# Cross attention: another order of its five slots

## What is computed

```python
def _L0_xattn_ref(query, key, value, Wq, bq, Wk, bk, Wv, bv, Wo, bo):
    q = (query @ Wq.T + bq).reshape(b, -1, H, HD).transpose(0, 2, 1, 3)
    k = (key @ Wk.T + bk).reshape(b, -1, H, HD).transpose(0, 2, 1, 3)
    v = (value @ Wv.T + bv).reshape(b, -1, H, HD).transpose(0, 2, 1, 3)
    scores = jnp.einsum('bhqd,bhkd->bhqk', q, k) / jnp.sqrt(jnp.float32(HD))
    attn = jax.nn.softmax(scores, axis=-1)
    out = jnp.einsum('bhqk,bhkd->bhqd', attn, v)
    out = out.transpose(0, 2, 1, 3).reshape(b, -1, D)
    return out @ Wo.T + bo
...
x = x + _L0_xattn_ref(_layernorm(x, axis=-1), ctx_1024, ctx_1024, L0_xattn_Wq, L0_xattn_bq, L0_xattn_Wk, L0_xattn_bk, L0_xattn_Wv, L0_xattn_bv, L0_xattn_Wo, L0_xattn_bo)
...
```

## Time and profile before

| | us |
|---|---|
| median of 3 runs | 3766.26 (3761.07 to 3767.85) |
| the profiled execution, own time | 3766.18 |
| its span | 3764.2 |
| the eight iterations of cross attention | about 77 to 629 of the span |
| one middle iteration | 71.69 |

### The profile page before, as it was taken

How to read it: one execution, slowest core, us unless ns; L and a number is a source line. 1 busy time by engine, 2 the same in 40 slices (tenths; PEclk the granted TensorE clock), 3 DMA queues, 4 the chain that set the end, 5 groups by cost and what they waited for, 6 DMA issues and landing times. The chain is left out here.

```text
span 3764.2 us, 57324 instructions
## 1 busy us (share of the span) xinstructions
PE 3529.5 (94%) x21008; PEld 2858.3 (76%) x21008; DVE 2305.5 (61%) x5002; ACT 1523.1 (40%) x3973; POOL 1185.7 (31%) x1044
## 2 busy tenths in 40 slices
PE   5889987899999997999999969999999699999998
PEld 4666665688888885888888858888888588888887
DVE  4776775799999994333323239999999642223231
ACT  4655663455555553211111125555555431111111
POOL 2333342455555540111111125555555111111111
PEclk8999999899999998999999989999999899999999
DMA  4111122212221114111111131222111221111111
GB/s 130 39 40 53 60 71 70 97 60 62 69 65 61 60 46 142 66 62 62 62 62 62 51 106 49 65 66 61 60 60 57 88 92 65 64 64 64 64 65 56
DMA packets 220778, 253.72 MB, mean 67 GB/s; under 512 B 33337, under 2 KB 147778, under 8 KB 220501
## 3 DMA queue, kind: packets, MB, share of 16 engines
q1 hardware_dynamic: 220501, 250.07, 20.4%
HBM read 142.62 MB, written 90.61 MB: 62 GB/s over the span
## 5 line engine op out<-in xcount | busy, mean ns | idle before, releaser
L1691 DVE SCALAR_TENSOR_TENSOR u_full<-banks,b_cols,gate 128x512 f32<-128x512 f32 (+1 forms) x176 | 132.1, 750 | 889.3 <-ACT gate L1633 792.8
L45 PE MATMUL banks<-fxT_h,w_h 128*128 128x512 f32 (+1 forms) x1408 | 558.2, 396 | 4.9 <-DVE fxT_l L1683 4.9
L47 PE MATMUL banks<-fxT_h,w_l 128*128 128x512 f32 (+1 forms) x1408 | 557.6, 396 | 0.0
L46 PE MATMUL banks<-fxT_l,w_h 128*128 128x512 f32 (+1 forms) x1408 | 556.3, 395 | 0.0
L1633 ACT ACTIVATE gate<-banks,b_cols 128x512 f32<-128x512 f32 (+1 forms) x176 | 121.2, 689 | 1028.7 <-PE banks L47 1028.7
L1021 POOL TENSOR_TENSOR rn<-ssq,neg_half 128x8 f32<-128x8 f32 x128 | 210.8, 1647 | 424.3 <-DVE ssq L1295 417.6
L45 PE MATMUL banks<-wqkv_h,hT_h 128*128 128x512 f32 x768 | 322.6, 420 | 16.4 <-DVE wqkv_l L1282 16.4
L1230 ACT ACTIVATE pT_h<-banks 128x384 fp32r<-128x384 f32 x512 | 223.8, 489 | 277.1 <-PE banks L1118 276.7
L1339 DVE TENSOR_SCALAR prob<-prob,rc 128x384 f32<-128x384 f32 x512 | 324.3, 675 | 9.1
L45 PEld LDWEIGHTS banks<-fxT_h,w_h 128*128 128x128 f32 (+1 forms) x1408 | 260.5, 185 | 75.5 <-DVE fxT_l L1683 10.9
L1223 ACT ACTIVATE prob<-neg_s,neg_m 128x384 f32<-128x384 f32 x512 | 310.9, 617 | 6.8 <-DVE neg_m L1327 6.8
(11 more groups left out here) (174 smaller groups left out, 8326.6 us busy)
## 6 DMA issues: line engine op xcount, KB each, us to landing
y_in<-y_rows SPq DMA_DIRECT2D x64, 256.0 KB, 3.0
z_rows<-y_in SPq DMA_DIRECT2D x64, 256.0 KB, 2.0
f_res<-z_rows SPq DMA_DIRECT2D x16, 1024.0 KB, 5.7
f_x<-x_rows SPq DMA_DIRECT2D x16, 1024.0 KB, 8.1
y_rows<-f_res SPq DMA_DIRECT2D x16, 1024.0 KB, 4.3
out_rows<-f_x SPq DMA_DIRECT2D x16, 1024.0 KB, 4.8
w_ffn_stage<-in_w SPq DMA_DIRECT2D x30, 512.0 KB, 4.6
x_in<-in_x SPq DMA_DIRECT2D x10, 1024.0 KB, 6.7
```

The costliest lines, as they stand in the source:

```text
L45: pe.matmul(out, a_h, b_h, start=start, stop=False)
L46: pe.matmul(out, a_h, b_l, start=False, stop=False)
L47: return pe.matmul(out, a_l, b_h, start=False, stop=stop)
L1691: e.scalar_tensor_tensor(out=u_full[r, m % 2, :], in0=ps[r, 2 * (m % 2), :], scalar=b1[r, m, 0:1], in1=gate[r, :], op0=ALU.add, op1=ALU.mu ...
```

## The change

The same instructions are issued, in another order within the slots, on four engines:

- TensorE: `queries(2)` moves from slot (0, 3) to (0, 1), and the four `project` each one slot later, to (0, 2), (0, 3), (0, 4), (1, 0) (the last stays); `queries(3)` moves from (1, 3) to (1, 1), and the next iteration's `queries(0)` and `queries(1)` from (2, 3) and (3, 3) to (2, 1) and (3, 1). The four `transpose_x` move from (1, 4), (2, 0), (2, 1), (2, 2) to (1, 2), (1, 3), (1, 4), (2, 0).
- ScalarE: `hi_p` always stands ahead of `exps` of its slot; `hi_q` moves from the end of slot 3 to the head of slot 2.
- VectorE: `lo_o` stands ahead of the maximum in slot 1 and `lo_q` ahead of that of slot 2; `moments` moves from (3, 0), (3, 2) to (3, 2), (3, 4), `normalise` from (0, 4), (1, 2) to (0, 1), (0, 2), `finish` from (1, 3), (1, 4) to (1, 4), (2, 1), `add_x1` and `moments_y` by up to a slot.
- GpSimd: `root` stands ahead of the first division of an iteration.

```diff
@@ tensor
-                            if (q, k) == (0, 1) and not g.first:
+                            if (q, k) == (0, 1):
+                                queries(2, q_out(2))
+                            elif (q, k) == (0, 2) and not g.first:
...
-                            elif (q, k) == (1, 3):
+                            elif (q, k) == (1, 1):
                                 queries(3, q_out(3) if g.first else w_out(4))
...
-                            elif (q, k) == (2, 3) and not g.last:
+                            elif (q, k) == (2, 1) and not g.last:
                                 queries(0, x_out(4))
-                            elif (q, k) == (3, 3) and not g.last:
+                            elif (q, k) == (3, 1) and not g.last:
                                 queries(1, q_out(5))
@@ scalar
-                            if k == 0 and q != 2 and more:
-                                exps(it, q + 1, k)
                             if k == 1 and not (g.first and q == 0):
                                 hi_o(it, q - 1)
+                            if k == 2 and (q < 2 or not g.last):
+                                hi_q(it, q + 2)
                             hi_p(it, QK * q + k)
...
+                            if k < GT and more:
                                 exps(it, q + 1, k)
-                            if k == 3 and (q < 2 or not g.last):
-                                hi_q(it, q + 2)
@@ vector
-                            if (q, k) in ((1, 3), (1, 4)) and old:
-                                for tt in ((0, 1) if k == 3 else (2, 3)):
+                            if (q, k) in ((1, 4), (2, 1)) and old:
+                                for tt in ((0, 1) if q == 1 else (2, 3)):
                                     finish(it - 1, g.slot(-1), tt)
-                            if q == DC - 1 and k in (0, 2) and not g.last:
-                                moments(g.slot(2), g.round(2), (0, 1) if k == 0 else (2, 3))
+                            if q == DC - 1 and k in (2, 4) and not g.last:
+                                moments(g.slot(2), g.round(2), (0, 1) if k == 2 else (2, 3))
```

More of the change, by code:

```diff
@@ L444, in body @@
                 def body(g, s):
+                    if not (g.first or g.last):
+                        root(g.it + 1)
                     for q in range(DC):
@@ L450, in body @@
                                 add_bias(g.it + 1, g.slot(1), 2 * (q - 2) + k)
-                            if q == 0 and k == 0 and not (g.first or g.last):
-                                root(g.it + 1)
                             if q == 1 and k == 1 and not g.first:
@@ L584, in body @@
                                 values(it, m - 2)
-                            if (q, k) == (1, 4) and not g.last:
-                                transpose_x(it + 1, 0, TURNS, q_out(4))
                 def nothing():
@@ L762, in body @@
                         for k in range(QK):
-                            x1_of = {(0, 2): 0, (0, 3): 1, (1, 0): 2, (1, 1): 3}.get((q, k))
+                            x1_of = {(0, 3): 0, (0, 4): 1, (1, 0): 2, (1, 1): 3}.get((q, k))
                             if x1_of is not None and old:
                                 add_x1(it - 1, g.slot(-1), x1_of, TURNS)
-                            if k == 1 and q == 0 and old:
+                            if k == 1 and (q or old):
                                 lo_o(it, q - 1)
+                            if k == 2 and (q < 2 or not g.last):
+                                lo_q(it, q + 2)
                             if k < GT and more:
                                 maxima(it, q + 1, k)
-                            if k == 1 and q:
-                                lo_o(it, q - 1)
                             if 0 < k < GT and more:
@@ L775, in body @@
                             lo_p(it, QK * q + k)
[L776 to L789, removed]
-                            if (q, k) in ((1, 3), (1, 4)) and old:
-                                for tt in ((0, 1) if k == 3 else (2, 3)):
+                            if (q, k) in ((1, 2), (1, 3), (1, 4), (2, 0)) and not g.last:
+                                lo_x(it + 1, {(1, 2): 0, (1, 3): 1, (1, 4): 2, (2, 0): 3}[q, k], TURNS)
+                            if k == 3 and more:
+                                recip(it, q + 1, 3)
+                            if (q, k) in ((0, 1), (0, 2)) and not g.last:
+                                normalise(it + 1, g.slot(1), (0, 1) if k == 1 else (2, 3))
+                            if x1_of is not None and old:
+                                moments_y(it - 1, g.slot(-1), x1_of)
+                            if (q, k) in ((1, 4), (2, 1)) and old:
+                                for tt in ((0, 1) if q == 1 else (2, 3)):
                                     finish(it - 1, g.slot(-1), tt)
-                            if q == DC - 1 and k in (0, 2) and not g.last:
-                                moments(g.slot(2), g.round(2), (0, 1) if k == 0 else (2, 3))
+                            if q == DC - 1 and k in (2, 4) and not g.last:
+                                moments(g.slot(2), g.round(2), (0, 1) if k == 2 else (2, 3))
                     assert g.last or own[0] == (OWN_FIRST if g.first else OWN), own[0]
```

22 lines of the change are left out of this document (10 added, 12 removed).

## The result

The changed kernel takes 3786.4 us (median of 6 runs, 3782.37 to 3791.97), the kernel before 3766.66 in the same comparison (6 runs, 3761.07 to 3770.39). The ratio is 1.0053, with a 95% interval of 1.004 to 1.0066. It is slower by 19.7 us; the forecast was 12.2 slower, at 3778.4 in a range of 3758 to 3792. The profiled execution spans 3786.8 us (own time 3788.59).

The account below looks back on a forecast made before the run. Every engine has slack in cross attention; TensorE loses 13.5 of 71.7 us per middle iteration to waits and clock. Middle iterations -3.0, first +2.0, last +1.6, keys +11.6 on 3766.18 gave 3778.4, range 3758 to 3792.

Parts of the forecast that it names:

- T + 9.5: Iteration's head: `project(0)` starts 9.5 us after T, the iteration's first transposes; 2.65 lost, against 1.6 before.
- E + 8.6: Fourth quarter's tail: transposes come 8.6 us after E, here the end of `queries(1)`; 3.25 us lost.
- A dense product (2.87) now lies between: Each quarter: a 2.87 us product covers the eviction of `xoT`, removing waits of 2.03 in (3, 2) and 1.35 in (0, 1).
- T + 2.75: Iteration's head: VectorE's first negation meets `root` (1.02 us) on GpSimd and ends 2.75 us after the first transposes, T.
- Transposes at E + 9.0: Third quarter's tail: first transposes come 9.0 us after E, the end of issue of `queries(0)`; 3.65 us lost.
- `hi_q` at E + 0.7, `lo_q` 1.5: Third quarter: `hi_q` comes 0.7 and `lo_q` 1.5 us after E, the end of issue of `queries(0)`.
- ends at E + 1.4: Third quarter: the last pair of `finish`, behind a GpSimd division, ends 1.4 us after `queries(0)` is issued.
- the term of the middle iteration: Losses of a middle iteration, 13.05 us against 13.5 before: a gain of about 0.5 each, 3.0 for six.
- 5.8 each: Two iterations with key loads: 5.3 us of new wait plus 0.5 for a fallen clock, 5.8 twice, +11.6.
- Faster: Rival: tails as short as the last iteration's, waits below 2.5 us each; -10.0, 3756 us; chance 0.13.
- Keys in time: Rival of no difference: the keys land before their scores, or cost up to 1.5 each; 3767 to 3770; chance 0.22.
- Clock stays low: Much slower rival: clock low behind long waits slows first-quarter products, 2 us more in seven iterations; 3792; chance 0.15.

Follow-up runs that it names:

- e1_keys_early: Changed kernel with the first half of the key loads issued right behind the store of `x_rows`, ahead of the wait for `finish`: 3766.68 us, ratio 1.0018.
- e4_hi_p_first: Kernel before with one part of the change alone, ScalarE's `hi_p` ahead of `exps` in slot 0: 3743.32 us, ratio 0.995.
- e2_q_slot3: Changed kernel with `queries(0)` and `queries(1)` and their evictions back in slots (2, 3) and (3, 3): 3779.27 us, ratio 1.0049.
- e5_bias_last: Changed kernel with GpSimd's four `add_bias` put behind the last division of each quarter: 3782.1 us, ratio 1.0048.
- e7_changed_mended: Changed kernel with first half of keys issued early, `add_bias` behind the last divisions and first half of `moments` in (3, 0): 3762.57 us, ratio 1.0004.
- e9_one_query_early: e4_hi_p_first with only `queries(1)` and its eviction moved, to slots (3, 1) and (3, 2): 3748.21 us, ratio 0.9956 to the kernel before.
- e8_before_moments_next: e4_hi_p_first with keys early and all `moments` in slot (0, 1) of the next iteration: 3735.87 us, ratio 0.9928 to the kernel before.

## Why the prediction was right, and where it was off

**Right in sign and in what waits.** The waits for `xoT_l` in (3, 2) and (0, 1) and for `xqT_l` at the head went, as said. The negation in the third quarter's last tile is held by the bias (1.24 and 1.23; 0.17 in the fourth quarter's, where the forecast had none either). The head was walked to `project(0)` at T + 9.5 and is at 9.26. The fourth quarter's transposes were put at E + 8.6, E the end of `queries(1)`; they stand at 8.43 (278.54 to 286.97); the wait there is 2.77, a little under the 3 of the forecast's list. The wait for keys was put at 8.5 and is 8.7; from `finish` to the scores 12.3 us pass, for 12.2. e1_keys_early shows this last mechanism to be 13 of the 20 us.

**The reason given for `xoT` was not the one that counted.** "A dense product (2.87) now lies between" was to cover these waits. e4_hi_p_first moves no product and has 2.9 us of them left of 20.9; e2_q_slot3 takes the products of the third and fourth quarter away again and has none in them. What suffices is the eviction `xpT` ahead of the four exponentials on ScalarE, which the forecast did not name as a gain. The waits went as forecast, in part by luck; whether the product would have covered them without the new order on ScalarE, no run shows.

**At the head, `root` does not hold the negation.** The walk had the first negation meet `root` and end at T + 2.75. It runs inside `root` and is not held:

```profile
289.17 0.17 DVE L713 TENSOR_SCALAR x_nmx<-x_mx 128x4 f32<-128x4 f32 x1
...
288.51 1.02 POOL L426 TENSOR_TENSOR x_rs<-x_ve,neg_half 128x4 f32<-128x4 f32 x1 [1.60 <-DVE x_ve L689]
```

It ends at T + 2.37; the 0.24 by which `project(0)` comes early may be this.

**Third quarter, mis-sized.** "Transposes at E + 9.0" measured 9.88 (`queries(0)` ends at 261.12). The step that failed is "`hi_q` at E + 0.7, `lo_q` 1.5": I let the two `y_t` ahead of `lo_q` be held by the division alone ("ends at E + 1.4"). They take 2.51 or 2.52, inside a division and a bias, and `lo_q` starts at E + 2.4. What bore on this was in the earlier trace rows for the negation beside the bias, and I did not apply it to the larger operations of the same kind. In e5_bias_last, where no bias meets it, this pair takes 1.54 (254.90) and `lo_q` starts at E + 1.8. With 0.9 more there, 0.2 less in each of the other two walks, and the slow clock costing 1.5 behind the tail for the 1.4 assumed (4.15 us from 271.00 to the next transposes, where 2.61 pass at full clock from 365.16; it falls mostly on values, not on `queries(1)`), the term of the middle iteration is -0.5 + 0.6 = +0.1; measured +0.1. That it closes is partly luck: the 2.1 of small waits was not walked again, and TensorE's waits at `transpose_x` sum to 7.2 us in seven iterations, 1.0 in each, for 1.9 in the walk.

**The keys, mis-sized.** "Ends at E + 1.4" for `finish` measured E + 2.49 (332.95 to 335.44), by the same 2.52. So keys come 1.1 later than forecast, of which 0.9 is hidden by the later tail, and the scores behind the long wait run at half clock (1.08 from scores to transposes, for about 0.7). 5.8 each became 6.5, shown by e1_keys_early at 6.6.

**The second, the first and the last iteration.** The second has 72.99 against 71.78 before, 1.2 more where -0.5 was said. Its slow spell begins with the head's transposes, which take 1.11 instead of 0.66, and here `project(0)` stands 10.44 behind them (142.19 to 152.63):

```profile
152.63 0.47 PE L45 MATMUL banks<-xwo_h,xoT_h 128*128 128x512 f32 x1 [0.43 <-DVE xqT_l L703]
```

The first has 63.65 against 60.33 (said: +2.0), the last is 2.3 longer (said: +1.6). In the trace of e1_keys_early the first iteration, the same code, is 62.36 long, 2.0 more than before: a slow spell falls otherwise from one execution to the next, and 1.3 of the first iteration's size is that (its last quarter is 17.17 long at a granted clock of 0.80 after the change, 15.74 at 0.91 in e1_keys_early).

**The sum.** In the profiled execution: second to seventh iteration 1.5 + 13.0 where 8.6 was said (+5.9), first +1.3, last +0.7, together 7.9 more than 12.2, that is 20.1; the medians differ by 19.7. The rest of the spans' 22.6 lies where the code is the same (1.5 before the first iteration, 1.1 behind the last), and the profiled execution is 2.2 above its median. The measured change is 1.6 times the forecast's, and 3786.4 lies just inside the band called "as forecast" (3771 to 3787).

**The rivals.** *Faster* asked for tails under 2.5: they are 3.14 and 2.77, and even at 2.34 to 2.47 with early keys (e7_changed_mended) the order is level with before. *Keys in time* would have been true with the loads ahead of the wait for `finish`; that is e1_keys_early. *Clock stays low* happened once, in the second iteration, at 1.2 us. In the others a spell comes behind the head's transposes, and `project(0)` stands at 9.26 with it (286.97) and without it (365.16 to 374.42), since it must wait for `xqT_l` either way.

**What stays open.** What eats the 0.5% that e4_hi_p_first gains: `queries(1)` alone accounts for little of it (e9_one_query_early), and the change's other parts (`hi_q` and `lo_q` in slot 2, `normalise`, `root` and `add_x1`, `queries(2)` ahead of the `project` products) were never run alone. The 13 us of the keys are shown by an experiment; that the rest is the bare tails is not.

## What to carry to other kernels

Before an instruction is moved, follow what waits behind it on its own queue, DMA queue included: here 13 of 20 us came from key loads that stood behind transfers that waited for a normalisation moved by two slots. A dense product is a cover for one gap at a time; moved here from the tail of a softmax to an earlier slot, it won nothing (e2_q_slot3, e9_one_query_early), and what won was to shorten the chain (four exponentials taken out from ahead of an eviction: 0.5%, against nothing for the products). Work of VectorE that GpSimd was seen to hold has to be priced by GpSimd's whole instruction whenever the two can meet; which pairs hold each other is read from the trace, pair by pair.

## What was not expected of the hardware

**VectorE held for whole instructions of GpSimd.** A pair of `y_t` (one input, 128x512) takes 1.00 alone, 1.54 beside a division (e5_bias_last, 254.90) and 2.51 to 2.52 across a division and a bias; a negation of 128x4 takes 0.17 alone and 1.23 to 1.25 beside a bias. Maxima, reciprocals and low halves beside GpSimd keep their time, and GpSimd's bias is longer too beside a pair of `y_t`, 1.48 for 1.28. The Trainium skill (SBUF — State Buffer, SBUF: two separate sides) says that GpSimd and a VectorE instruction in a 2-port mode take the shared port pair as an exclusive lock for a whole instruction, and that the other blocks. The trace agrees for the bias: the negation ends 0.03 us after it (339.63 and 339.60). It does not agree for `root`: a negation that starts inside it takes 0.17 and ends before it, at every meeting in these traces (289.17 in 288.51 to 289.53 after the change). Here the measurement decides: beside `root` nothing was held.

**A small load behind other transfers lands late.** The last key load of the half needs 5.8 us from issue to landing, before and after the change, with `x_in`, `y_rows` and `y_late` issued just ahead. Behind the store of `x_rows` alone, in e1_keys_early, it needs 1.9. The Trainium skill (DMA: Bandwidth & Descriptors, Anatomy of one DMA) has 2.0 us fixed for a DMA of the GpSimd path; by that figure the forecast would have been 3770, and the measured 12.3 from `finish` to the scores sides with the row. The 1.9 of e1_keys_early, for loads issued by SyncE, is near that figure.

**A spell at 1.2 GHz costs nothing where the time is lost anyway.** Behind the head's wait of 2.77 us matmuls run at half clock for some 3 us, and the next wait behind them shrinks from 2.00 to 0.47; `project(0)` does not move. Begun a little sooner, with the head's transposes in the second iteration, it does cost: 1.2 us more to `project(0)`, which then waits 0.43. Nor is a spell certain behind a given wait: one of 1.74 at `transpose_x` had one behind it in the kernel before, and in e8_before_moments_next the same wait, 1.73 at 237.60, has none in a window whose clock is 1.00.
